# Label projection of a pair of graphs as one Strassen product, in a graph network layer on one core

## The reference

```python
# x = hid: 64 graphs, 128 nodes, 256 features; adj: 0 or 1 here; D = 4 labels
mask = (adj[None] == labels[:, None, None, None]).astype(dt)
weight = mask / (jnp.sum(mask, axis=-1, keepdims=True) + EPS)
agg = jnp.einsum('dbmn,bnh->bmdh', weight, hid).reshape(B, N, D * H)
out = relu(agg @ Wd.T + bd)
r = sigmoid(out @ Wri.T + bri + hid @ Wrh.T + brh)
z = sigmoid(out @ Wzi.T + bzi + hid @ Wzh.T + bzh)
n = tanh(out @ Wni.T + bni + r * (hid @ Wnh.T + bnh))
out = (1 - z) * n + z * hid
return layernorm(out) * gamma + beta
```

## Time and profile before

| | |
|---|---|
| median of 3 runs | 529.98 us (529.72 to 530.1) |
| the profiled execution | 530.06 us, of which span 528.2 us |
| PE busy | 510.0 us (97%), 3035 matmuls |
| DVE busy | 432.0 us (82%) |
| ACT busy | 387.3 us (73%) |
| POOL busy | 297.2 us (56%) |
| DMA | 63 GB/s mean |

### The profile page before, as it was taken

How to read it: one execution, slowest core, us unless ns; L and a number is a source line. 1 busy time by engine, 2 the same in 40 slices (tenths; PEclk the granted TensorE clock), 3 DMA queues, 4 the chain that set the end, 5 groups by cost and what they waited for, 6 DMA issues and landing times.

```text
span 528.2 us, 10541 instructions
## 1 busy us (share of the span) xinstructions
PE 510.0 (97%) x3035; PEld 464.1 (88%) x3035; DVE 432.0 (82%) x1073; ACT 387.3 (73%) x733; POOL 297.2 (56%) x308
## 2 busy tenths in 40 slices
PE   8989899999999999999999999999999999999992
PEld 3777799999999999999999999999999999999992
DVE  4886788888887888888888888888888888888777
ACT  4848777777777777777777777787777787777682
POOL 2757565555656654656555565665565556555325
PEclk9999999999999999999999999999999999999997
DMA  8230121022122012122102212211212220210111
GB/s 299 90 120 2 50 71 55 37 71 70 51 72 69 37 53 69 50 69 69 61 28 69 69 50 69 69 48 41 69 51 68 69 69 25 65 40 21 40 43 60
DMA packets 20262, 33.42 MB, mean 63 GB/s; under 512 B 2257, under 2 KB 6993, under 8 KB 20241
## 3 DMA queue, kind: packets, MB, share of 16 engines
q1 hardware_dynamic: 19872, 32.38, 19.2%
q10 hardware_dynamic: 288, 0.52, 0.4%
q0 software_dynamic: 80, 0.26, 0.1%
HBM read 24.77 MB, written 8.39 MB: 63 GB/s over the span
## 4 chain that ended last, share of the span: by engine, by line
PE 89%; DVE 5%; ACT 2%; issue 2%; DMA 1%; POOL 1%; POOLq 0%; ACTq 0%; DVEq 0%
PE y_bank L359 32%; PE alpha L359 24%; PE gamma L359 12%; PE p_bank L396 11%; PE beta L359 6%; PE t_bank L404 3%; DMA shared<-in_wdT 1%; PE t_bank L385 1%; DVE y_lo L984 1%; DVE wx_lo L979 1%; DVE masks L966 0%; DVE wd_lo L990 0%; ACT wx_hi L676 0%; POOL shared L1514 0%; ACT x_hi L707 0%
## 5 line engine op out<-in xcount | busy, mean ns | idle before, releaser
L1436 POOL TENSOR_TENSOR x_lo<-x_f,x_hi 128x1024 fp32r<-128x1024 f32 x29 | 76.0, 2621 | 85.8 <-ACT x_hi L785 85.8
L741 ACT ACTIVATE y_hi<-y_bank 128x512 fp32r<-128x512 f32 x120 | 72.0, 600 | 57.0 <-PE y_bank L359 57.0
L359 PE MATMUL y_bank<-wd_hi,x_hi 128*128 128x512 f32 x252 | 101.7, 403 | 0.0
L359 PE MATMUL y_bank<-wd_lo,x_hi 128*128 128x512 f32 x252 | 99.7, 396 | 0.0
L359 PE MATMUL y_bank<-wd_hi,x_lo 128*128 128x512 f32 x252 | 99.3, 394 | 0.0
L1060 DVE TENSOR_TENSOR y_lo<-y_bank,y_hi 128x512 fp32r<-128x512 f32 x120 | 81.7, 681 | 4.2 <-ACT y_hi L741 4.0
L396 PE MATMUL p_bank<-y_hi,masks 128*128 128x256 f32 x256 | 67.0, 284 | 4.9 <-issue 3.1
L1471 POOL TENSOR_TENSOR o_lo<-o_sums,o_hi 128x512 fp32r<-128x512 f32 x30 | 38.8, 1293 | 50.3 <-ACT o_hi L837 50.3
L396 PE MATMUL p_bank<-y_lo,masks 128*128 128x256 f32 x256 | 66.3, 281 | 0.0
L749 ACT ACTIVATE p_bank<-p_bank,ratio 128x256 f32<-128x256 f32 x120 | 49.2, 458 | 10.8 <-PE p_bank L396 10.8
L359 PEld LDWEIGHTS y_bank<-wd_lo,x_hi 128*128 128x128 f32 x252 | 47.3, 188 | 10.9
(11 more groups left out here) (244 smaller groups left out, 1405.0 us busy)
## 6 DMA issues: line engine op xcount, KB each, us to landing
x_f<-in_xT SPq DMA_DIRECT2D x32, 256.0 KB, 2.6
x_rows<-in_x SPq DMA_DIRECT2D x32, 256.0 KB, 3.1
out<-shared SPq DMA_DIRECT2D x31, 256.0 KB, 2.0
adj_in<-in_adjT SPq DMA_DIRECT2D x32, 128.0 KB, 2.4
shared<-in_wgT SPq DMA_DIRECT2D x2, 576.0 KB, 6.3
shared<-in_wdT ACTq DMA_DIRECT2D x2, 256.0 KB, 5.2
vec_rows<-in_vectors SPq DMA_DIRECT2D x1, 512.0 KB, 6.6
shared<-in_wgT SPq DMA_DIRECT2D x2, 192.0 KB, 7.1
```

The lines of the kernel that those rows point to most:

```text
L359: done = nc.tensor.matmul(dst, m, w, start=(first and t == 0), stop=(last and t == 2), skip_group_check=inside)
L741: nc.scalar.activation(y_hi[:, g, half(b)], y_bank[b][:, :], ACT.Copy)\
L1436: nc.gpsimd.tensor_tensor(*split_lo(x_lo[:, k % XRING, :, :], x_f[:, k % 2, :, :], x_hi[:, k % XRING, :, :])).then_inc(xlo_ready, 1)
```

## The change

y of a pair becomes seven block products: the same sums of x, and sums T1 to T4 of the blocks of Wd.T, made once at the start (four subtractions on POOL, four copies on ACT, four subtractions on DVE). The first two y steps (2 and 3) keep the old form (`step`), the 28 steps 4 to 31 take the new one (`fast_step`). The scheme's partial results need copies and additions: ACT copies y_alpha to beta, u2_y and u3_y, and DVE adds y_gamma to the latter two in SBUF. y_hi is then read from PSUM for two blocks and from SBUF for two, and the remainders of the SBUF ones move from DVE to POOL. ACT's rectification of three blocks of t_bank goes away; DVE's instructions that read them rectify on the fly.

```diff
+            def fast_step(i, up):          # PE
+                pe.wait_ge(yl21_ready, up(n - 1))
+                y_product(y_alpha, A11, B11, True).then_inc(yp1_done, 1)
+                product(alpha, A11, B11).then_inc(p1_done, 1)
+                pe.wait_ge(p_scaled, up(4 * i, 4))
+                p_products(i - 1, 1, True)
+                pe.wait_ge(y11_seeded, up(n))
+                y_product(y_alpha, S2, T2).then_inc(yp6_done, 1)
+                y_product(beta, A12, B21).then_inc(yp2_done, 1)
+                pe.wait_ge(out_ready, up(2 * i, 2))
+                transposes()
+                product(gamma, S1, T1).then_inc(p5_done, 1)
+                y_product(y_alpha, S3, T3).then_inc(yp7_done, 1)
+                y_product(y_gamma, S1, T1, True).then_inc(yp5_done, 1)
+                pe.wait_ge(beta_seeded, up(q + 1))
+                product(alpha, S2, T2).then_inc(p6_done, 1)
+                product(beta, A12, B21).then_inc(p2_done, 1)
+                y_product(y_alpha, A22, T4).then_inc(yp4_done, 1)
+                pe.wait_ge(u2_ready, up(q))
+                product(alpha, S3, T3).then_inc(p7_done, 1)
+                y_product(y_gamma, S4, B22).then_inc(yp3_done, 1)
+                pe.wait_ge(yl21_ready, up(n))
+                pe.wait_ge(yl22_ready, up(n))
+                p_products(i, 0, False)
+                product(alpha, A22, T4).then_inc(p4_done, 1)
+                pe.wait_ge(p_scaled, up(4 * i + 2, 4))
+                p_products(i, 0, True)
+                product(gamma, S4, B22).then_inc(p3_done, 1)
+                counted(i + 1)
+                pe.wait_ge(yl11_ready, up(n))
+                pe.wait_ge(yl12_ready, up(n))
+                p_products(i, 1, False)
...
+            def fast_step(i, up):          # ACT
+                scale(i - 1, 1)
+                    nc.scalar.activation(x_hi[:, k % XRING, :, :], x_f[:, k % 2, :, :], ACT.Copy).then_inc(xhi_ready, 1)
+                nc.scalar.activation(beta[:, :], y_alpha[:, :], ACT.Copy).then_inc(y11_seeded, 1)
...
+            def fast_step(i, up):          # DVE
+                dve.wait_ge(rz_ready, up(m + 1))
+                nc.vector.tensor_tensor(mix[:, :].rearrange("p (g j f) -> p g j f", g=2, j=2), c_sb[:, :, :, 0:128],
+                                        rz_sb[:, :, 0, :].rearrange("p g (j f) -> p g j f", j=2), ALU.mult)\
+                    .then_inc(rn_ready, 1)
+                nc.vector.tensor_tensor(u3_y[:, :], y_gamma[:, :], u3_y[:, :], ALU.add).then_inc(y22_ready, 1)
+                    make_masks(i + 1, up(16 * ((i + 1) // 2 + 1), 8))
+                nc.vector.tensor_tensor(mix[:, :], z_part[:, :], n_sb[:, :], ALU.add).then_inc(mix_ready, 1)
...
-                    nc.scalar.activation(t_bank[:, N:4 * N], t_bank[:, N:4 * N], ACT.Relu).then_inc(relu_ready, 1)
-                    nc.vector.tensor_tensor(o_sums[:, S1 - 3, :], o_sums[:, A21, :], blocks[:, A22, :], ALU.add)\
+                    nc.vector.scalar_tensor_tensor(o_sums[:, S1 - 3, :], blocks[:, A22, :], 0.0, o_sums[:, A21, :],
+                                                   ALU.max, ALU.add).then_inc(osum_ready, 1)
```

More of the change, by code:

```diff
@@ L101, in gnn_kernel @@
         n_sb = later(7168, 1)
+        u2_y, u3_y = later(7680, 1), later(4608, 1)
         from_n = later(5120, 1)
@@ L121, in gnn_kernel @@
         more_vec = x_rows[:, 0, :, :].rearrange("p g f -> p (g f)")
+        wd_sum_of = {w: x_rows[:, place, :, :].rearrange("p g f -> p (g f)") for w, place in ((T3, 1), (T1, 0), (T2, 0), (T4, 1))}
         y_bank = [bank("y_bank0"), bank("y_bank1")]
+        y_alpha, y_gamma = y_bank
         p_bank = bank("p_bank")
@@ L652, in _ @@
             head()
-            run_steps(pe, step)
+            run_steps(pe, step, fast_step)
             tail()
@@ L724, in head @@
                 act.wait_ge(ohi_ready, 1)
-                nc.scalar.activation(t_bank[:, :], t_bank[:, :], ACT.Relu).then_inc(relu_ready, 2)
+                nc.scalar.activation(t_bank[:, :], t_bank[:, :], ACT.Relu).then_inc(relu_ready, 1)
                 y_high(1, 1, 1)
@@ L956, in _ @@
             head()
-            run_steps(act, step)
+            run_steps(act, step, fast_step)
             tail()
@@ L1372, in _ @@
             head()
-            run_steps(dve, step)
+            run_steps(dve, step, fast_step)
             tail()
@@ L1483, in step, with fast_step @@
                     nc.gpsimd.tensor_tensor(rstd[:, :], var_eps[:, :], power[:, :], ALU.pow).then_inc(rstd_ready, 1)
+            def fast_step(i, up):
+                m, n = i - LAG_MIX, i - YS + 1
+                if n == 1:
+                    sum_blocks(i + 1, up, 16 * ((i + 1) // 2 + 1))
+                if has_pair(i + 1):
+                    k = i + 1
+                    pool.wait_ge(xhi_ready, up(k - 1))
+                    nc.gpsimd.tensor_tensor(*split_lo(x_lo[:, k % XRING, :, :], x_f[:, k % 2, :, :],
+                                                      x_hi[:, k % XRING, :, :])).then_inc(xlo_ready, 1)
+                if has_pair(i + 2):
+                    sum_blocks(i + 2, up, up(16 * ((i + 2) // 2 + 1), 8))
+                pool.wait_ge(tanh_ready, up(m + 1))
+                pool.wait_ge(rows_loaded[m % 2], up(16 * (m // 2 + 1), 8))
+                pool.wait_ge(zpart_ready, up(m))
+                nc.gpsimd.tensor_tensor(from_n[:, :], x_rows[:, m % 2, :, :].rearrange("p g f -> p (g f)"), n_sb[:, :],
+                                        ALU.subtract).then_inc(from_ready, 1)
+                pool.wait_ge(from_ready, up(m + 1))
+                pool.wait_ge(mix_ready, up(m))
+                nc.gpsimd.tensor_tensor(z_part[:, :].rearrange("p (g f) -> p g f", g=2), rz_sb[:, :, 1, :],
+                                        from_n[:, :].rearrange("p (g f) -> p g f", g=2), ALU.mult).then_inc(zpart_ready, 1)
+                pool.wait_ge(yh22_ready, up(n))
+                nc.gpsimd.tensor_tensor(*split_lo(y_lo[:, EVEN, half(1)], u3_y[:, :], y_hi[:, EVEN, half(1)]))\
+                    .then_inc(yl22_ready, 1)
+                pool.wait_ge(oshi_ready, up(i))
+                pool.wait_ge(p3_done, up(i - 2))
+                nc.gpsimd.tensor_tensor(*split_lo(o_lo[:, (i - 1) % 2, 3:7, :], o_sums[:, 1:5, :],
+                                                  o_hi[:, (i - 1) % 2, 3:7, :])).then_inc(oslo_ready, 1)
+                pool.wait_ge(mv_ready, up(2 * m + 2, 2))
+                nc.gpsimd.tensor_tensor(var_eps[:, :], mean_var[:, :, 1], ln_eps[:, :], ALU.add).then_inc(ve_ready, 1)
+                pool.wait_ge(result_ready, up(2 * m, 2))
+                pool.wait_ge(ve_ready, up(m + 1))
+                nc.gpsimd.tensor_tensor(rstd[:, :], var_eps[:, :], power[:, :], ALU.pow).then_inc(rstd_ready, 1)
+                pool.wait_ge(yh12_ready, up(n))
+                nc.gpsimd.tensor_tensor(*split_lo(y_lo[:, ODD, half(1)], u2_y[:, :], y_hi[:, ODD, half(1)]))\
+                    .then_inc(yl12_ready, 1)
```

335 lines of the change are left out of this document (300 added, 35 removed).

## The result

The changed kernel takes 645.01 us (median of 4 runs, 643.82 to 645.9), the kernel before 530.04 in the same series: a ratio of 1.217 (1.214 to 1.219). It is slower, as predicted, by 115 us where 91 were predicted, and 5 us above the upper end of the range. Its profiled execution has a span of 642.5 us, 114.3 more than before.

What follows compares the result with a forecast made beforehand. PE alone was taken to bound the kernel, at 15.56 us a step. 14.86 plus waits of 0.42, 0.19, 3.18, 0.15 and 0.10 gave 18.9; 530 + 90 + 1 = 621 us, range 548 to 640.

Steps and rivals of the forecast that it cites:

- the largest term: PE's wait for DVE's y_alpha remainder, after masks and mix addition alternate with POOL instructions: 3.18 us a step.
- The start: Extra 128x512 instructions on POOL, ACT and DVE, and an extra pair's sums ahead of x_lo: +1 us, bounds -1 and +4.
- the port: SBUF port of DVE and POOL, locked for a whole instruction; masks and POOL were to alternate, PE waiting 3.18 us.
- about 1.0: Sign to look for: DVE's L1489, held up under POOL's x_lo, takes about 1.0 us in place of 0.69.
- The bound from above: Cost of a mask that comes second at the port: the rest of the POOL instruction; from below, nothing.
- the ratio of 1.94: DVE's 4-column ratio in the first steps, both inputs in SBUF: 1.94 us, standing still until POOL's x_lo was through.
- Above 640 (0.02): Rival, chance 0.02: PE's long idle time each step lets its granted clock fall, slowing the work behind; time above 640.
- the small waits: PE's waits in each step besides the 3.18 us one: 0.42, 0.19, 0.15 and 0.10 us.
- PE for y11_seeded (0.42): First wait of a step: PE waits for ACT's copy of y_alpha to beta, behind scale and x_hi, 0.42 us.
- The two at the end: PE's waits at the step's end: 0.15 us for scaling, 0.10 for POOL's y_lo of u2_y.
- The first two waits: PE waits 0.42 us for y11_seeded, then 0.19 for ACT's copy to beta ahead of S2·T2.
- The 0.70 that PE saves: Seven block products of y in place of eight on PE: 0.70 us a step, 19.6 us in 28 steps.

Runs made afterwards that it cites:

- experiment 3: Changed kernel plus ten products of zeros into p_bank on PE, ahead of its wait for the y_alpha remainder; 624.84 us, ratio 1.178.
- Experiment 1: Changed kernel with POOL's y_lo of u3_y made to wait until DVE's mix addition is done; 563.46 us, ratio 1.063.
- Experiment 2: Changed kernel with the new steps' masks in the form that also writes a sum, POOL's instructions left in place; 576.2 us, ratio 1.087.
- Experiment 4: Changed kernel with ACT's copy of y_alpha to beta moved ahead of x_hi; 658.24 us, ratio 1.244.
- Experiment 11: Changed kernel with y_lo waiting for the mix, sum-writing masks, ACT, POOL, DVE and PE reordered, gamma's bias loaded ahead of scaling, T4 split early; 532.59 us, ratio 1.0048.

## Where the prediction held, and which step of it failed

The mechanism of the largest term held. The time is 24 us above the forecast and 5 above the range because of a term that the sum put at nothing: the fall of the granted clock behind PE's new wait, 22 us. The start adds 4.4 more than was put down, and the port costs 3.9 less.

**Where the 114.3 us lie.** The ratio of step 4 starts at 66.98 us before and at 70.28 after: 3.3. The first new step takes 22.17 in place of 15.36: 6.8. The next 26 take 19.56 in place of 15.57: 103.7. The tail adds 0.5.

**The port, the largest term: right.** The prediction laid the step out from the end of the last label products; that is 326.72 in the step shown. Measured against forecast: the masks ask at 8.1 (8.4); z_part ends at 9.1 (9.2), y_lo at 10.4 (10.6), o_lo at 11.7 (12.0); the mix addition ends at 12.7 (13.1), L1533 at 14.1 (14.5); PE starts at 14.13, and with the 0.27 by which its group is longer it is back at 14.40 (14.85). Behind each of the three POOL instructions one mask is let in, the third with nothing of POOL's behind it, and the fourth follows at once. The 128x128 instructions for o that rectify take 0.28, where 0.06 had been added to 0.29; the masks ask 0.3 earlier by it, still under z_part, so nothing is gained. The step at full clock is 18.76, as experiment 3 shows, against 18.9: 27 times 3.19 is 86.1 us, where 90 were put down. Experiment 1 is the proof: with y_lo and o_lo put behind the mix, the masks take 1.82. Experiment 2 is the other: masks that don't use the port, and only the mix addition is late. L1489 took 1.02 of "about 1.0". The bound from above, the rest of the POOL instruction, was the right one to take, since the only row of an instruction coming second (the ratio of 1.94) was of that kind.

**The clock: the step that failed.** "Above 640 (0.02): PE's long idle time each step lets its granted clock fall". This was not rare: it came in most steps. The sum held a wait of 3.18 us in each step and priced PE behind it at full speed, and the prediction gave no reason for the small chance. Granted clock (the number behind the busy times) in four stretches right behind three such waits, which ended at 340.85, 301.28 (two stretches) and 321.07; in the first it did not fall:

```profile
340.00:346.00 6.00, 5.03 (x35) 4.41 (x36) 4.68 (x13) 2.80 (x6) 2.21 (x3) 1.00 0.23 65
...
302.00:304.00 2.00, 2.00 (x8) 2.00 (x8) 0.55 (x1) 1.36 (x3) 0.86 (x2) 0.50 0.11 43
304.00:306.00 2.00, 2.00 (x12) 1.84 (x11) 0.97 (x2) 1.20 (x2) 0.93 (x1) 0.69 0.00 0
322.00:324.00 2.00, 2.00 (x10) 1.92 (x10) 0.35 (x1) 1.97 (x5) 0.93 (x2) 0.57 0.01 5
```

1.00 is the higher of the two levels, 2.4 GHz, and 0.50 the lower, 1.2 GHz. The chain shows what that does to PE's groups; the product of 1.05 takes 1.92, the next label products 0.85 for 0.47:

```profile
300.55 0.69 DVE y_lo L1533
...
301.28 0.81 PE p_bank L447 x4
302.09 1.92 PE alpha L410 x6
304.01 0.85 PE p_bank L447 x4
304.86 1.27 PE gamma L410 x6
```

In 7 of the 27 distances the step is 18.4 to 18.8 us, in the other 20, the first new step among them, it is 19.7 or more. Experiment 3 leaves all other engines as they are and fills PE's idle time with zeros: the 26 steps behind the first new one take 18.47 to 18.94, and the time is 20 us less. By it the fall costs 0.80 a step on average over the 26, 20.8 us, and 1.3 in the first (22.17 against 20.88). Without it the time would be about 625, inside the range and 4 from the forecast. Experiments 1 and 2 bear it out from the other side: without the long wait their mean granted clock is 0.99. The profile before could have told this. In its tail PE works last at 518.4 us, and the granted clock is 1.00 over 518 to 520, 0.89 over 520 to 522 and 0.50 from there on: it fell two to four us into the idleness, about the length of the wait that was forecast.

```profile
518.00:520.00 2.00, 0.37 (x3) 0.05 (x1) 2.00 (x8) 0.00 (x0) 1.22 (x2) 1.00 0.00 0
520.00:522.00 2.00, 0.00 (x0) 0.00 (x0) 1.75 (x8) 0.69 (x2) 1.57 (x5) 0.89 0.34 131
522.00:524.00 2.00, 0.00 (x0) 0.00 (x0) 1.83 (x6) 0.84 (x2) 0.63 (x2) 0.50 0.00 0
```

The Trainium skill, TensorE: Matmul & The Clock Gate, "Part 1: The HAM clock gate (the "warmup" mystery)", has the clock fall to 1.2 GHz after idleness; the trace agrees (0.50 in the stretch from 302 us, behind 2.4 us of it).

**The start: too small.** Predicted +1, bounds -1 and +4. Measured: 3.3 until the first new step and, with the clock's part taken off, 20.88 - 18.76 = 2.1 in it: 5.4, above the upper bound. The split of this step between clock and start is good to some tenths only, since in experiment 3 the clock fell in it too, at another place:

```profile
75.00:78.50 3.50, 3.50 (x13) 3.20 (x12) 3.47 (x4) 2.98 (x6) 3.25 (x4) 0.51 0.32 88
```

In experiment 1 it fell nowhere in this step, and there the first new step is 18.45 - 16.57 = 1.9 longer. The prediction saw that the first new step adds up an extra pair ahead of x_lo, but not who stands behind it: ACT's x_hi waits 1.85 us, the copy to beta is behind x_hi on ACT, and PE waits for that copy.

```profile
71.63 1.06 ACT L1004 ACTIVATE x_hi<-x_f 128x1024 fp32r<-128x1024 f32 x1 [1.85 <-POOL x_f L1738]
72.59 0.58 ACT L1008 ACTIVATE beta<-y_bank 128x512 f32<-128x512 f32 x1
```

```profile
73.22 0.50 PE L410 MATMUL y_bank<-wdt_hi,x_hi 128*128 128x512 f32 x1 [1.77 <-ACT beta L1008]
```

T4's split lies on the same chain: ACT makes its high part (L1015, at 73.62) behind the copy to beta, and DVE's remainder, under x_lo, takes 1.43 in place of 0.68 and holds up L1489 behind it. What each of the two costs in this order was not tried.

```profile
74.27 1.43 DVE L1484 TENSOR_TENSOR wd_lo<-x_rows,wd_hi 128x512 fp32r<-128x512 f32 x1 [1.77 <-ACT wd_hi L1015]
```

Of the 3.3 us ahead of it, the chain from 28 to 70 us now holds DVE's remainders of T1 to T3 (L1195) and of wx; which of the new instructions costs what there was not tried.

**The sum again.** The port and the small waits 86.1, the clock 20.8 + 1.3, the start 5.4, the tail 0.5, and 0.2 because step 4 of before was 15.36: 114.3. The forecast had 90 + 1.

**PE for y11_seeded (0.42): right in size, but not to be had back alone.** The weight loads wait 12.0 us in 27 times, 0.44 each. Experiment 4 removes this wait and costs 13 us, since the next hand-over was in line behind it.

**Inside the step, two errors that cancel.** PE's last product ahead of the port's wait ends at 11.70 (11.67), so this wait is 2.70 where 3.18 was put down. The two at the end are larger than their 0.15 and 0.10, by these rows of the chain:

```profile
342.63 0.68 PE p_bank L447 x4
...
344.37 0.20 PE t_bank L436 x8
...
344.69 0.75 PE p_bank L447 x4
```

The label products behind scaling follow their forerunner without a gap and take 0.68 for 0.47, 0.21 more; those of the second graph end 0.87 behind the counts, 0.40 more. They were not tested by themselves. The first two waits are about 0.4 and 0.2, as forecast, and 14.86 with all five makes the 18.8 of this step. That 18.76 came so near 18.9 is in part luck: 0.5 too much for the port, 0.36 too little for the end.

**The 0.70 that PE saves: right, and reachable in large part.** Experiment 11 has a step of 15.44 against 15.57, with all cures in it. 14.86 of it are full matmuls, and 0.58 are waits and slower groups behind them: the four groups of the rows of experiment 11 are longer by 0.18, 0.11, 0.19 and 0.15, about that together. It is slower than before only by its start: 26 steps of 0.13 give back 3.4 us, the start costs 3.4 and 1.2. No kernel that was tried beats the one before. Whether a step nearer to 14.86 can be had, and with it a faster kernel, stays open.
